# Last attention: the scores two units ahead issued first in each unit, ahead of the fill and the turn

## What is computed

```python
q = (hidden_states @ q_proj_w.T).reshape(B, Q, NUM_HEADS, HEAD_DIM).transpose(0, 2, 1, 3)
k = (cross_attention_states @ k_proj_w.T).reshape(B, KV, NUM_KV_HEADS, HEAD_DIM).transpose(0, 2, 1, 3)
v = (cross_attention_states @ v_proj_w.T).reshape(B, KV, NUM_KV_HEADS, HEAD_DIM).transpose(0, 2, 1, 3)
q = rmsnorm(q, q_norm_w)
k = rmsnorm(jnp.repeat(k, n_rep, axis=1), k_norm_w)
v = jnp.repeat(v, n_rep, axis=1)
scores = jnp.einsum('bhqd,bhkd->bhqk', q, k) * scale + attention_mask
attn = jax.nn.softmax(scores, axis=-1)
out = jnp.einsum('bhqk,bhkd->bhqd', attn, v)
return out.transpose(0, 2, 1, 3).reshape(B, Q, NUM_HEADS * HEAD_DIM) @ o_proj_w.T
```

## Time and profile before

| | |
|---|---|
| median of 3 runs | 949.99 us (947.75 to 950.53) |
| the profiled execution, its own time | 950.46 us |
| its span in the profile | 948.8 us |
| last attention, first turn of rows to last step | about 294 to 839 us of the span |
| TensorE matmul busy | 803.6 us, 85% |
| TensorE weight load busy | 653.8 us, 69% |
| VectorE busy | 735.3 us, 77% |
| ScalarE busy | 524.1 us, 55% |
| GpSimd busy | 451.4 us, 48% |
| mean granted clock of TensorE | 0.937 of full speed |

### The profile page before, as it was taken

The page is one execution under the profiler, slowest core; times in us unless marked ns, Lnnn a source line. Parts: engine busy times, 40 slices in busy tenths (PEclk is TensorE's granted clock), DMA queues, the critical chain, the costliest instruction groups (busy, mean ns, idle before and its releaser), DMA issues. The chain is left out here.

```text
span 948.8 us, 16522 instructions
## 1 busy us (share of the span) xinstructions
PE 803.6 (85%) x5158; PEld 653.8 (69%) x5158; DVE 735.3 (77%) x1719; ACT 524.1 (55%) x1414; POOL 451.4 (48%) x389
## 2 busy tenths in 40 slices
PE   0886686774678899999999999999999998787578
PEld 0365465552347789889889988898898897653246
DVE  8784876876864788788888797887887888649964
ACT  6564586764425755675676657657655756431220
POOL 4646158803102574673755745745746636333010
PEclk9888997997789999999999999999999998998879
DMA  8323136407011031120210220220302102030001
GB/s 326 109 79 130 37 134 227 161 1 246 0 45 46 9 108 42 50 84 22 89 46 20 89 66 0 89 66 14 119 22 73 60 22 66 23 108 1 0 1 44
DMA packets 37001, 68.22 MB, mean 72 GB/s; under 512 B 5665, under 2 KB 15457, under 8 KB 36834
## 3 DMA queue, kind: packets, MB, share of 16 engines
q1 hardware_dynamic: 36962, 67.73, 21.4%
HBM read 62.38 MB, written 5.34 MB: 71 GB/s over the span
## 5 line engine op out<-in xcount | busy, mean ns | idle before, releaser
L2127 DVE TENSOR_SCALAR_CACHE_REDUCE xn<-ctxT,candidate 128x512 bf16<-128x512 f32 x248 | 174.4, 740 | 0.0
L1894 ACT ACTIVATE layer_attention_probs<-xnT,stats 128x512 f32<-128x512 f32 x128 | 94.1, 735 | 130.3 <-DVE stats L1997 130.3
L1680 PE MATMUL bank<-layer_attention_keysT,layer_attention_queriesT 128*128 128x512 f32 x384 | 122.5, 428 | 3.2 <-DVE layer_attention_queriesT L1990 3.1
L2009 DVE TENSOR_TENSOR layer_attention_probsT<-bank,layer_attention_probsT 128x512 fp32r<-128x512 f32 x128 | 88.2, 689 | 46.3 <-ACT layer_attention_probsT L1902 44.8
L1680 PEld LDWEIGHTS bank<-layer_attention_probsT,layer_attention_values 128*128 128x128 f32 x768 | 100.6, 192 | 15.8 <-DVE layer_attention_probsT L2009 6.1
L1680 PE MATMUL bank<-layer_attention_probsT,layer_attention_values 128*128 128x256 f32 x768 | 103.9, 285 | 7.4 <-DVE layer_attention_probsT L2009 6.8
L1680 PE MATMUL bank<-layer_attention_wo,layer_attention_headsT 128*128 128x512 f32 x384 | 102.2, 409 | 2.9 <-issue 2.9
L1902 ACT CAST layer_attention_probsT<-bank 128x512 fp32r<-128x512 f32 x128 | 74.8, 584 | 52.4 <-PE bank L1751 52.4
L1680 PE MATMUL bank<-layer_attention_l_wkv,layer_context_parts 128*128 128x256 f32 x768 | 100.5, 283 | 0.0
L1680 PEld LDWEIGHTS bank<-layer_attention_l_wkv,layer_context_parts 128*128 128x128 f32 x768 | 97.8, 190 | 2.5
L1680 PE MATMUL bank<-layer_attention_l_wq,layer_attention_xnT 128*128 128x512 f32 x384 | 93.2, 392 | 0.0
(11 more groups left out here) (313 smaller groups left out, 1738.2 us busy)
## 6 DMA issues: line engine op xcount, KB each, us to landing
layer_attention_l_raw_qo<-in_wqT SPq DMA_DIRECT2D x9, 1024.0 KB, 5.0
xnT<-inverse_sums SPq DMA_DIRECT2D x16, 512.0 KB, 3.8
layer_attention_l_raw_qo<-in_woT SPq DMA_DIRECT2D x8, 1024.0 KB, 7.1
tw_raw<-in_w_gateT SPq DMA_DIRECT2D x8, 688.0 KB, 5.2
tw_raw<-in_w_upT SPq DMA_DIRECT2D x8, 688.0 KB, 4.1
tw_raw<-in_w_downT SPq DMA_DIRECT2D x6, 768.0 KB, 4.8
layer_attention_l_raw_kv<-in_wkvT SPq DMA_DIRECT2D x9, 512.0 KB, 5.0
ternary<-tw_rounded SPq DMA_DIRECT2D x8, 344.0 KB, 2.5
```

Source lines behind the costliest of these rows:

```text
L1680: last = pe.matmul(out, stationary[f][a], moving[f][b], start=f == 0 and x == 0, stop=f == count - 1 and x == 2)
L1894: a.activation(probs[:, u % 3, :], masked[:, u % 2, :], ACT.Exp, bias=negmax[:, u:u + 1], scale=-1.0, accum_out=sums[:, u:u + 1]).then_inc ...
L2009: v.tensor_tensor(probsT[:, 1, p % 2, :, columns], T[u % 2][:, :].rearrange("p (c q) -> p c q", c=CPB), probsT[:, 0, p % 2, :, columns], A ...
L2127: own(k.nc.vector.tensor_scalar(k.flags[:, r % 2], row_tile(k.ctxT, r), k.candidate[:, r:r + 1].bitcast(F32), 0.0, ALU.is_ge, ALU.add, acc ...
```

## The change

In TensorE's `run`, within each unit, the `scores` of two units ahead move from behind the fill and the turn of the probabilities to the front of the unit. Nothing is added or taken away, and no wait's target changes.

```diff
@@ -1791,12 +1791,12 @@
                 def run(step, first=False, last=False):
                     following, before = after(step), after(step, -1)
                     for u in range(UNITS):
-                        fill(step, u, first, last)
-                        turn_probs(step, u)
                         if u + 2 < UNITS:
                             scores(step, u + 2)
                         elif not last:
                             scores(following, u + 2 - UNITS)
+                        fill(step, u, first, last)
+                        turn_probs(step, u)
                         if u == 0 and not first:
                             mix(before, PAIRS - 1)
                         if u == 2:
```

## The result

The changed kernel takes **1015.45 us** (median of 4 runs, 1011.17 to 1015.83) against 950.26 us for the kernel before, measured beside it (4 runs, 947.75 to 952.59): 1.068 times as long, 95% interval 1.064 to 1.072. The profiled execution took 1015.76 us with a span of 1014.0 us, 65.2 us more than the span before. The same work ran: VectorE, ScalarE and GpSimd are busy as long as before to within 3 us. TensorE's matmuls are busy for 14.5 us more (803.6 before, 818.1 now); the other 50.7 us are time in which TensorE has nothing to run.

A forecast was written before the change was run, and what follows sets the result against it. TensorE, busy 20.00 of 20 us, was taken to set the pace. Added waits of 61.2 us, less 4.5 and 3.0 given back, plus 5.3 for the clock, made 59.0: 1009.0 us, range 985 to 1046.

The forecast's parts named there:

- The holes: Gaps on TensorE before moved scores whose input is late; forecast at units 5, 6 and 7, each adding its length.
- Unit 7 and odd unit 6: Following step's scores wait for the low part of the queries, through ScalarE and VectorE: 1.74 us at each place.
- Even unit 6: In even steps a weight split delays ScalarE's rounding, so the following step's scores wait longer: 2.69 us.
- Odd unit 5: In odd steps the scores of unit 7 wait for unit 5's maximum, late behind a long VectorE operation: 0.69 us.
- Step 0: Already waits in units 6 and 7; only its turns come from under the wait, adding 1.0 us.
- The clock: TensorE's clock falls to 0.50 behind half of the seven long even-step gaps: 5.3 us added.
- Given back: Waits for the low part of the probabilities shrink by 4.5 us, and 3.0 us of low clock goes.
- Short queues: Rival: ScalarE and VectorE never late for turned rows; even steps 1.74, odd unit 5 none; 992 us, chance 0.20.
- Clock: Rival: three gaps within 10 us lower the clock repeatedly, 21 more falls of 1.5 us; 1040 us, chance 0.12.
- Head start: Rival: early scores let maxima and exponentials run ahead, removing 6.8 us of waits; 940 us, chance 0.03.
- Slack in the engine: Rival: TensorE catches up in the 9% without weight loads, 45 us, leaving 14; 964 us, chance 0.04.

The follow-up runs named there:

- e8: Kernel before, with VectorE's last low part of the probabilities moved from the next step's start to ahead of the bisection update: 947.88 us, ratio 0.995.
- e9: The change, with only the first half of ScalarE's query weight split in even steps moved from unit 5 to unit 6: 999.6 us, ratio 1.051.
- e2: Kernel before, with scores first only in units 6 and 7, where they belong to the following step: 996.62 us, ratio 1.047.
- e3: Kernel before, with scores first in unit 7 only: 971.88 us, ratio 1.022.
- e4: Kernel before, with scores first in unit 6 only: 978.79 us, ratio 1.027.
- e10: Kernel before, with scores first in units 0 to 3 only and the old order in units 4 to 7: 952.31 us, ratio 1.002.
- e1: Kernel before, with scores first in units 0 to 5 only, where they belong to the same step: 963.79 us, ratio 1.014.
- e5: The change, with both halves of ScalarE's query weight split in even steps moved one unit later: 1030.04 us, ratio 1.084.
- e7: Kernel before, with the turn of rows put ahead of the mix in units 5 and 6: 954.53 us, ratio 1.003.
- e6: The change, with the turn of rows put ahead of the mix in units 5 and 6: 999.63 us, ratio 1.050.

## Why the prediction was right

It said 1009.0 with a range of 985 to 1046, against 1015.45. The direction, the mechanism and the places were right. That the number came within 6.45 us is in part luck, since the terms missed in both directions: beside the 59.0 of the forecast, the pairs of steps added 5.0 us less, while step 0 and the falls of the clock added 2.2 and 3.8 more and 5.2 less was given back, 6.2 in sum.

- **The holes.** Unit 7 and odd unit 6: 1.74 predicted, 1.73 measured. Even unit 6: 2.69 predicted, 2.60 measured; the chain was right, but the mix ahead takes 1.49 and not 1.40, so TensorE comes later. Odd unit 5: 0.69 predicted, 0.51 measured; TensorE comes 0.09 later than was reckoned, and the scores start 0.05 after the maximum's end (433.73 + 0.08 = 433.81, start 433.86) and not the 0.15 taken from the low part of the queries. A pair of steps: 8.60 predicted, 7.89 measured, of which 7 x 7.89 = 55.2 against 60.2. The holes themselves are 0.51 + 3 x 1.73 + 2.60 = 8.30, or 58.1 in seven pairs.
- **What the earlier trace rows did not show.** Most of the other 0.41 us of a pair is a wait that the kernel before had in unit 0 of the odd steps (3 to 11; steps 1 and 13 have it in the waits view), and that the modelled ends hide in TensorE's matmul row:

```profile
534.13 0.94 PE L1680 MATMUL bank<-layer_attention_keysT,layer_attention_queriesT 128*128 128x512 f32 x3
534.44 0.68 DVE L2009 TENSOR_TENSOR layer_attention_probsT<-bank,layer_attention_probsT 128x512 fp32r<-128x512 f32 x1
535.17 1.47 PEld L1680 LDWEIGHTS bank<-layer_attention_probsT,layer_attention_values 128*128 128x128 f32 x12 [0.53 <-DVE layer_attention_probsT L2009]
```

From the scores to the mix it is 1.04 (535.17 - 534.13) instead of 0.78, and the mix then takes 1.52 instead of 1.41. Without that wait a pair takes 65.70 (e8), 0.38 less. The hole of unit 7 gives VectorE the time and the wait is gone, so these 0.38 us a pair, some 2.5 in all, belong to what is given back. The new lengths of blocks nearly cancel: scores behind a mix take 0.70 instead of 0.78 and six output matmuls behind scores 1.39 instead of 1.47, but a mix behind a turn takes 1.49 instead of 1.40.

- **Step 0** was too small: 1.0 predicted, 3.2 measured (the turn of keys in step 1 starts at 357.38, not at 354.15). Of this, 0.55 is there at the first turn of rows already (294.24 against 293.69), before any block that moved. For the rest the step "only its turns come from under the wait" failed. The chain to the waiting scores hangs on the turn of unit 4, which in step 0 comes 1.50 later (320.15 against 318.65): 0.55 of the start, 0.78 for one more block of scores ahead of it, and a wait of 0.16 for a maximum. And the clock stays at 0.50 into 333, behind 3.50 us of idleness, twice as long as in the earlier trace rows:

```profile
327.91 1.62 PE L1680 MATMUL bank<-layer_attention_keysT,layer_attention_queriesT 128*128 128x512 f32 x3 [3.50 <-DVE layer_attention_queriesT L1990]
```

- **The clock** fell behind six of seven long holes, not behind half: 9.1 against 5.3. The cost of one, 1.5, was right.
- **Given back** was the worst term: 7.5 taken, 2.3 measured (55.2 + 3.2 + 9.1 = 67.5, less the 65.2 by which the end is later), or about 4.8 with the 2.5 us that lie inside the pairs. The waits in the waits view fell by 2.7 only (6.8 to 4.1), and half of that is the wait of 1.37 at the start of step 13. The wait for the low part of the probabilities at the start of step 15 did shrink to 1.13, where 1.0 was predicted, and the clock stayed up there. But most of the time was spent again: further into step 15 an idle stretch of 2.62 us, released by a maximum, brings the clock down after all. From `turn_rows` of the second query tile in step 14 to the first instruction behind the attention (L2295) it is 47.11 before (793.64 to 840.75) and 47.62 now (858.65 to 906.27), so with the hole of 1.73 in front of it step 15 gave back 1.2 us.

```profile
880.16 1.63 PE L1680 MATMUL bank<-layer_attention_keysT,layer_attention_queriesT 128*128 128x512 f32 x3 [2.62 <-DVE stats L1997]
...
880.00:883.00 3.00, 2.83 (x7) 2.25 (x8) 1.41 (x5) 1.49 (x4) 0.00 (x0) 0.54 0.00 0
```

Why step 15 answers in this way was read from the trace alone; no run isolates it. e8 has the like at the same step.

**The rivals.** *Short queues* fell: the even hole is 2.60, and e9, which shortens ScalarE's queue in front of it, brings it to 1.76, the length that this rival gave it from the start. *Clock*: in steps 1 to 14 the falls come behind the long holes alone; the idle stretches of 1.49 to 1.65 us bring none, in the change and in e2, e3, e4 and e9. *Head start*: the maxima did not run ahead in any way that counts (e10). *Slack in the engine* fell too: a pair of steps is longer by 7.89 of its 8.30 us of holes, and most of what is missing is the short wait that is gone. The Trainium skill (Perfetto Trace Analysis, Identifying the Most-Contended Engine) judges TensorE's headroom by two figures, one of them the busy share of the weight loads, 91% in the earlier trace rows. Here the measurement decides against reading the other 9% as room: next to all of each hole came on top. The clock that stayed up behind 2.37 us in the earlier trace rows was the rarer case: in this stage it stayed up behind one stretch of that length in seven.

## What to carry to other kernels

On an engine that is full and takes its work in order, ask of every wait what the instructions between the producer's start and the wait are, and add up their lengths: that is the cover, and a block moved past it takes cover away at its old place and wherever its leaving brings the engine sooner to another wait (e1). A later place in another engine's queue is only free if nothing hangs on it, buffers that are to be loaded again above all (e5), and an earlier place on TensorE only if its bank has been read out (e7). A wait shorter than what the modelled ends hide is missing from the matmul row and can be looked for at the weight loads (e10). And a stall at the end of a stage that is "given back" has to be followed one wait further before it is counted (e8, and the 7.5 us of the forecast).

## What the runs showed of the hardware

- In steps 1 to 14, where TensorE is otherwise full, the clock fell only behind the longer idle stretches: those of 1.49 to 1.65 us, 14 to 28 in a run, never brought it down (e2, e3, e4, e9 and the change); those of 2.03 us did in three of seven (e6), those of 2.35 in six of seven (the change). The length alone does not settle it. In e5, stretches of 2.31, 2.54, 2.84, 2.85 and 2.89 us brought the clock down and those of 2.48 and 2.50 did not; at the start of step 15, 2.82 us brought it down in the kernel before, while 2.65 (e4) and 2.95 (e10) left it up. A fall costs 1.51 us of time in the change.
- A mix of twelve matmuls of 256 columns takes 1.40 us from start to start when scores stand ahead of it, and 1.49 when a turn does (474.17 - 472.68); scores take 0.70 behind a mix and 0.78 behind a turn. An order of the same instructions thus has its own length within some tenths of a microsecond a step.
